# Two attentions' first batch started ahead of the pipeline, its maxima over five banks, and a last expert that writes finished rows

## What is computed

```python
x = x + tanh(g_xattn[0]) * L0_xattn(layernorm(x), ctx, ctx, mask, ...)   # causal
x = x + tanh(g_ffn[0])   * L0_ffn(layernorm(x), ...)                     # 32 experts, top 8, capacity 256
x = x + tanh(g_xattn[1]) * L1_xattn(layernorm(x), ctx, ctx, mask, ...)   # not causal
x = x + tanh(g_ffn[1])   * L1_ffn(layernorm(x), ...)                     # 8 experts, top 2, capacity 1024

def xattn(q, k, v):
    att = softmax((q @ Wq + bq) @ (k @ Wk + bk).T / sqrt(16) + mask)     # per head
    return (att @ (v @ Wv + bv)) @ Wp + bp
def L1_ffn(x):
    for each expert e, for the up to 1024 tokens routed to it:
        y[token] += gate * (relu(x[token] @ w1[e] + b1[e]) @ w2[e] + b2[e])
```

## Time and profile before

| | |
|---|---|
| median of 3 executions | 2030.68 us (2028.8 to 2036.93) |
| the profiled execution | 2030.42 us |
| its span on the core | 2028.6 us |
| TensorE busy | 1761.9 us (87%) |
| VectorE busy | 1013.3 us (50%) |
| ScalarE busy | 886.9 us (44%) |
| GpSimd busy | 795.0 us (39%) |
| mean DMA rate | 110 GB/s |

### The profile page before, as it was taken

The page is one execution under the profiler, slowest core; times in us unless marked ns, Lnnn a source line. Parts: engine busy times, 40 slices in busy tenths (PEclk is TensorE's granted clock), DMA queues, the critical chain, the costliest instruction groups (busy, mean ns, idle before and its releaser), DMA issues. The chain is left out here.

```text
span 2028.6 us, 29697 instructions
## 1 busy us (share of the span) xinstructions
PE 1761.9 (87%) x10299; PEld 1053.1 (52%) x10299; DVE 1013.3 (50%) x2630; ACT 886.9 (44%) x1684; POOL 795.0 (39%) x772
## 2 busy tenths in 40 slices
PE   3799999998846998558999999999955999999995
PEld 1456556655535877423344444443332666666664
DVE  4556666667465544218777777777420122212221
ACT  3367666665622222132777777766731111111110
POOL 4222376665634777522121233111123234433322
PEclk8899999999978999887999999999976999999998
DMA  3535556344226888534323442331132133333314
GB/s 110 173 121 164 154 167 178 113 142 125 77 78 160 171 171 171 82 119 150 96 79 94 127 140 79 113 110 60 45 97 92 26 79 84 83 78 80 82 21 104
DMA packets 210675, 223.00 MB, mean 110 GB/s; under 512 B 39870, under 2 KB 201663, under 8 KB 209863
## 3 DMA queue, kind: packets, MB, share of 16 engines
q1 hardware_dynamic: 176746, 177.54, 29.0%
q0 software_dynamic: 33792, 43.71, 11.9%
HBM read 155.10 MB, written 87.06 MB: 119 GB/s over the span
## 5 line engine op out<-in xcount | busy, mean ns | idle before, releaser
L914 DVE TENSOR_REDUCE nmx<-mxb 128x1 f32<-128x512 f32 (+1 forms) x896 | 522.2, 609 | 253.7 <-PE mxb L685 147.2
L772 ACT ACTIVATE pt<-stb 128x512 f32<-128x512 f32 x832 | 475.0, 598 | 257.2 <-PE stb L705 128.9
L685 PE MATMUL mxb<-kst,qst 96*128 96x512 bf16 (+4 forms) x1024 | 335.3, 350 | 32.6 <-DVE nmx L914 21.5
L702 PE MATMUL stb<-qst,kst 99*128 99x512 bf16 (+4 forms) x1024 | 326.0, 343 | 7.1 <-DMA qst<-m3T 4.4
L718 PE MATMUL ob<-pt,va 128*32 128x512 f32 (+3 forms) x2048 | 219.4, 523 | 2.7 <-ACT pt L772 1.7
L1245 POOL DMA_INDIRECT slots<-number,place x192 | 189.5, 987 | 58.6 <-issue 57.9
L702 PEld LDWEIGHTS stb<-qst,kst 102*128 102x128 bf16 (+1 forms) x1024 | 99.1, 99 | 215.0 <-ACT pt L772 134.3
L1768 POOL DMA_INDIRECT x_after_l<-e_y,e_token x64 | 99.5, 1555 | 271.9 <-DVE e_y L1733 257.2
L1215 POOL TENSOR_TENSOR qk<-qk,parts 128x512 f32<-128x512 f32 x64 | 72.9, 1161 | 336.6 <-ACT qk L807 224.8
L685 PEld LDWEIGHTS mxb<-kst,qst 99*128 99x128 bf16 (+1 forms) x1024 | 101.4, 99 | 146.5 <-DVE nmx L914 73.4
L1531 POOL DMA_INDIRECT x_after_l<-e_y,token x64 | 104.4, 1631 | 46.9 <-DMA x_after_l<-e_y,token 19.8
(11 more groups left out here) (258 smaller groups left out, 2891.3 us busy)
## 6 DMA issues: line engine op xcount, KB each, us to landing
qk_parts<-parts SPq DMA_DIRECT2D x16, 1536.0 KB, 6.5
qst<-qk_parts SPq DMA_DIRECT2D x384, 64.0 KB, 2.3
kst<-qk_parts SPq DMA_DIRECT2D x384, 64.0 KB, 2.2
rows<-rows SPq DMA_DIRECT2D x15, 1060.0 KB
crow<-in_ctx SPq DMA_DIRECT2D x16, 512.0 KB, 3.8
x_after_l<-xres SPq DMA_DIRECT2D x16, 512.0 KB, 3.3
e_gu_nat<-in_L_ffn_gate_up_proj SPq DMA_DIRECT2D x64, 128.0 KB
qst<-in_L_ffn_w SPq DMA_DIRECT2D x8, 1024.0 KB, 7.3
```

The lines of the kernel that those rows point to most:

```text
L685: last = pe.matmul(out, qst[par][0:rows_used, h, qt * P:(qt + 1) * P], kst[par][0:rows_used, h, 0:nk], start=True, stop=not causal)
L702: last = pe.matmul(bank[:, to:to + S - q_from(kt)], kst[par][0:ROWS, h, kt * P:(kt + 1) * P], qst[par][0:ROWS, h, q_from(kt):S], start=Tru ...
L772: act.activation(pt[:, slot(b, u), q0:S], stb[no % N_ST][:, q0:S], ACT.Exp, scale=SCALE).then_inc(s["st_free"], 1)
L914: last = dve.tensor_reduce(nmx[:, qt, h:h + 1], got[:, at:at + k_to(qt)], AX.X, ALU.max, negate=True)
```

## The change

`ITERATIONS` starts at -2 in both attentions. All of batch 0's projections stand ahead of the pipeline, in the order c, k, x, q, v (`first` on TensorE, the calls before the loop on ScalarE); k gets two of the `stb` banks and q and v one `work` bank each. k's split is ScalarE's and GpSimd's as before, q's is ScalarE's and VectorE's (`split_first`). k's half of the parts is stored on its own, then q's (`first_store`), and each stack now reads k before q. All four stacks of batch 0 stand on SP right behind that, with batch 2's x behind the first. The first half of batch 0's shift moves from behind batch 1's second stack to behind its first.

The maxima of batch 0 go round five banks, the two of `mxb` and the three of `stb` (`max_bank`); the first score of an attention waits until all maxima of batch 0 are read (`EARLY`).

In layer 0 the loads come in the order k, biases, q, v; the gates are loaded by ScalarE's queue; the second pair of stacks' ones (`w_ones1`), the empty rows and batch 0's residual stand behind batch 0's stacks; VectorE does the statistics of batch 0 ahead of the constants and the bias after batch 1's statistics (`set_up_bias`), and GpSimd fills one of the three `va` tiles first.

In `experts1` the copy to the output starts when seven experts are added. For the last one GpSimd gathers the sums so far (`gather_sums`), VectorE adds them to the gated result in one instruction, and GpSimd writes finished rows into the output (`write`), after the copy has landed.

Before, eight adds (L1768) stood in the place of the last two rows. The core of the diff:

```diff
-        ITERATIONS = range(-3, B + 2)
+        ITERATIONS = range(-2, B + 2)
+        def max_bank(n, u):
+            i = MAX_NO[u]
+            if n == 0 and i < EARLY:
+                ring = (*mxb, *stb)
+                return ring[i % len(ring)], i - len(ring) + 1
+            return mxb[i % N_MX], N_MAX * n + i - N_MX + 1
...
+            def first_store():
+                for side, ready, stored in ((1, s["lo_k"], s["k_out"]), (0, s["lo_q"], s["parts_out"])):
+                    sp.wait_ge(ready, 1)
+                    sp.dma_start(qk_dram[0][side]..., parts[:, side, :, :, :]...).then_inc(stored, 16)
...
+            first_store()
+            for g in range(GROUPS):
+                stack(0, g)
+                if g == 0:
+                    load_x(2)
+            if layer == 0:
+                sp.dma_start(kst[1][ROW_SHIFT:ROW_SHIFT + 3, :, :], ones).then_inc(a.w_ones1, 16)
+                sp.dma_start(qst[1][ROW_MASK:ROW_MASK + 3, :, :], ones).then_inc(a.w_ones1, 16)
+                empty_store(c, sp, empty)
             load_residual(0)
...
                 if nn is not None:
                     parts_store(nn)
                     stack(nn, 0)
+                if nxt == 0:
+                    shift(nxt, 0)
...
+                if no == 0:
+                    pe.wait_ge(s["max_free"], EARLY)
...
+            def first():
+                for kind in ("c", "k", "x", "q", "v"):
+                    for t in range(2):
+                        for part in range(2 if kind in TWO_PARTS else 1):
+                            trip(kind, 0, t, part)
...
+            def split_first():
+                dve.wait_ge(evac["q"], 2)
+                dve.wait_ge(s["hi_q"], 1)
+                for cc in range(NC):
+                    last = dve.tensor_tensor(qk[:, 0, cc, :], qk[:, 0, cc, :], parts[:, 0, 0, cc, :], ALU.subtract)
+                last.then_inc(s["rest_q"], 1)
+                dve.wait_ge(s["mid_q"], 1)
+                for cc in range(NC):
+                    last = dve.tensor_tensor(parts[:, 0, 2, cc, :], qk[:, 0, cc, :], parts[:, 0, 1, cc, :], ALU.subtract)
+                last.then_inc(s["lo_q"], 1)
...
-            sp.wait_ge(s["added"], 16 * TILES * E1)
+            sp.wait_ge(s["added"], 16 * TILES * (E1 - 1))
             sp.dma_start(out, x[0:T, :]).then_inc(s["copied"], 16)
...
+            def gather_sums(b):
+                pool.wait_ge(s["picked"], at(2, b, 2))
+                pool.wait_ge(s["added"], 16 * TILES * (E1 - 1))
+                for i in range(TILES):
+                    pool.indirect_dma_start(sums[:, i, :], None, x, ...).then_inc(s["sum_in"], 16)
+            def write(b):
+                pool.wait_ge(s["copied"], 16)
+                for i in range(TILES):
+                    pool.wait_ge(s["y_done"], at(TILES, b, i + 1))
+                    pool.indirect_dma_start(out, ..., y[b[1]][:, i, :], None, ...).then_inc(s["written"], 16)
```

More of the change, by code:

```diff
@@ L542, in _ @@
                     load_ctx(nn + 1)
-                if n3 is not None and n3 + 1 < B:
+                if n3 is not None and 2 < n3 + 1 < B:
                     load_x(n3 + 1)
@@ L563, in _ @@
                     store_rows(prev)
+                if layer == 0 and cur == 0:
+                    sp.wait_ge(c.empty_out, 16)
                 if layer == 0 and cur is not None:
@@ L583, in bank_free @@
             def bank_free(kind, b, t):
-                bank = BANK[kind, t]
+                if kind == "k" and b == 0:
+                    return
+                bank = t if kind in ("q", "v") and b == 0 else BANK[kind, t]
                 if held[bank]:
@@ L734, in _ @@
                 pe.wait_ge(c.tables, 2)
-                pe.wait_ge(c.made, 3)
+            first()
+            if layer == 0:
+                set_up()
             for it in ITERATIONS:
@@ L755, in _ @@
                         kind, k, t, part, _ = TRIPS[u]
[L756 removed]
+                        if item(it, k) is not None and (kind != "list" or layer == 0 and item(it, k) >= LISTED) and (kind not in FRONT or item(it, k) > 0):
                             trip(kind, item(it, k), t, part)
@@ L796, in evacuate @@
                         act.wait_ge(a.va_ones, 1)
+                    if layer == 0 and t == 0 and 0 < b < 3:
+                        act.wait_ge(a.va_ones, b + 1)
                     if t == 0 and b > 2:
@@ L853, in _ @@
                 constants_scalar(c, act)
-                act.wait_ge(a.b_in, 32)
+            evacuate("c", 0, 0)
+            evacuate("c", 0, 1)
+            for i in range(NT):
+                norm1_apply(0, i)
+            evacuate("x", 0, 0)
+            evacuate("x", 0, 1)
+            if layer == 0:
+                act.wait_ge(a.b_in, 48)
+            evacuate("k", 0, 0)
+            evacuate("k", 0, 1)
+            evacuate("q", 0, 0)
+            evacuate("q", 0, 1)
+            middle(0, 1)
+            middle(0, 0)
+            evacuate("v", 0, 0)
+            evacuate("v", 0, 1)
             for it in ITERATIONS:
                 prev, cur, nxt, nn, n3 = (item(it, k) for k in range(-1, 4))
-                if layer == 0 and it == -1:
-                    act.wait_ge(a.w_ones, 64)
+                nn = nn or None
+                if layer == 0 and it == 0:
                     act.wait_ge(c.empty_out, 16)
@@ L1117, in _ @@
             if layer == 0:
+                dve.memset(c.mhalf[:, :], -0.5).then_inc(c.half_set, 1)
                 dve.memset(m3T[0][:, :], 1.0).then_inc(a.stack_ones, 1)
-                constants_vector(c, dve, ii, empty)
             else:
                 dve.memset(base[:, :, :], 0.0).then_inc(a.zeroed, 1)
+            for i in range(NT):
+                norm1_stats(0, i)
+            norm1_mean(0)
+            if layer == 0:
+                constants_vector(c, dve, ii, empty)
+                set_up()
+            split_first()
             for it in ITERATIONS:
                 done, prev, cur, nxt, nn, n3 = (item(it, k) for k in range(-2, 4))
-                if layer == 0 and it == -2:
-                    set_up()
                 for u in range(STEPS):
+                    if layer == 0 and it == -2 and u == 14:
+                        set_up_bias()
                     if nxt is not None and u in MAX_BANKS:
@@ L1249, in _ @@
                 constants_gpsimd(c, pool, ii)
+                pool.memset(va[0][:, :, :, :], 1.0).then_inc(a.va_ones, 1)
+            norm1(0)
+            rest(0, 1)
+            low(0, 1)
             for it in ITERATIONS:
-                if layer == 0 and it == -2:
-                    for i in range(3):
-                        last = pool.memset(va[i][:, :, :, :], 1.0)
-                    last.then_inc(a.va_ones, 1)
                 done, prev, nn, n3 = item(it, -2), item(it, -1), item(it, 2), item(it, 3)
+                nn = nn or None
                 for u in range(STEPS):
+                    if layer == 0 and it == -2 and u == 15:
+                        for i in range(1, 3):
+                            pool.memset(va[i][:, :, :, :], 1.0).then_inc(a.va_ones, 1)
                     if layer and done is not None and u in (0, 16, 18, 24):
@@ L1743, in iteration @@
                 hidden(cur, 1, (1, 3, 5, 7))
-                result(cur, 0)
+                result(cur, 0, not nxt)
                 if nxt:
@@ L1747, in iteration @@
                     hidden(nxt, 0, (1, 3, 5, 7))
-                result(cur, 1)
+                result(cur, 1, not nxt)
             pipeline(dve, E1, prologue, iteration)
@@ L1773, in iteration @@
                     gather(nxt)
-                add(cur)
+                    add(cur)
+                else:
+                    gather_sums(cur)
+                    write(cur)
             pipeline(pool, E1, gather, iteration)
-            pool.wait_ge(s["added"], 16 * TILES * E1)
+            pool.wait_ge(s["written"], 16 * TILES)
 def program(nc, a, out):
```

136 lines of the change are left out of this document (85 added, 51 removed).

## The result

The changed kernel took 1980.92 us (median of four runs, 1979.48 to 1982.58), the kernel before 2030.59 in the same job: the ratio is 0.9745, with a 95% interval from 0.9728 to 0.9761. That is 49.7 us less, where 53 were forecast.

A forecast was written before the change was run, and what follows sets the result against it. Chains bound both attention heads before first scores, and the result's copy ran alone at the end; TensorE bound from the first scores on. Gains 21.6 + 16.5 + 15.0 = 53.1 us gave 1977 us, range 1963 to 1992.

The forecast's parts named there:

- first attention, to the first scores: Head of the first attention: following SP's queue, first scores at 84.8 instead of 106.37, gain 21.6 us (15 to 30).
- second attention, block to first scores: Head of the second attention: maxima 9.0 us earlier, then 44.5 instead of 52.0 to first scores; gain 16.5 us.
- the end, from the second down projection of expert 8: Program's end: the result's copy runs under expert 8, saving 15.7 us and up to 1.6 more; 15.0 with the stall.
- stall: Under expert 8: wait for the gather of the sums, taken as 1.0 us, with ends 0 and 5.
- everything between, carried over: Iteration 0 to the last add: taken as unchanged; the forecast is wrong if these stretches change in length.
- the train: SP, first attention: ones, empty rows and residual stand ahead of batch 1's parts, which the first scores' shift waits for.
- Rival A: First attention: SP's queue doesn't bind, first scores at 77.3, 7.5 us earlier; 1970 us, chance 0.13.
- rival B: Second attention: the five banks give nothing because TensorE's projections stand between the maxima; 7.5 us later, 1985, chance 0.11.
- the upper bound: Program's end: up to 1.6 us more if a plain write is cheaper than an add; end's range 11 to 17.3.
- rival C: Program's end: the gather comes so late that TensorE stands for 6 us; 1982 us, chance 0.05.
- D: Both heads: the first stack starts no earlier, only the end's gain is left; 2015 us, chance 0.03.
- E: Both iterations 0: shorter heads leave TensorE at the lower of its two clocks; 2079 us, chance 0.02.

The follow-up runs named there:

- the two repeats: The changed kernel and the kernel before, each run once more unaltered: 1980.11 us and 2031.62 us (one run).
- e4: Changed kernel with the second pair of ones, the empty rows and batch 0's residual issued ahead of batch 0's parts in the first attention: 1976.64 us.
- e6: Changed kernel with batch 0's first shift behind batch 1's second stack again: 1988.11 us.
- e5: Changed kernel with batch 0's maxima in two banks again, without the first score's wait for all of them: 1987.39 us.
- e9: Changed kernel with the edits of e2, e4 and e8 (7 matmuls), and batch 1's statistics ahead of batch 0's q split: 1962.19 us.
- e8: Changed kernel with 20 additional matmuls whose result nobody reads, where TensorE stands idle in the second attention: 1974.41 us.
- e2: Changed kernel without GpSimd's drain at the end of the last block: 1977.08 us.
- e1: Changed kernel with the last block as before the change (the last expert adds, the copy follows all adds): 1993.65 us.

## Why the prediction was right, and where its terms were off

The forecast held in place and sign, and by 3.9 us in size. The terms, in us, by the two first profiles and by the two repeats:

| term | forecast | first pair | repeats |
|---|---|---|---|
| first attention, to the first scores | 21.6 | 20.5 | 21.5 |
| second attention, block to first scores | 16.5 | 13.5 | 16.8 |
| the end, from the second down projection of expert 8 | 15.0 (16.0, less 1.0 of stall) | 12.2, without the stall | 12.1, without the stall |
| everything between, carried over (the stall in it) | 0 | 2.8 | -1.6 |
| spans | 53.1 | 49.0 | 48.7 |

**First attention.** The forecast followed SP's queue, and each of its stations is in the trace: the first stack at 31.67 (31.5 forecast), the fourth stack over at 57.3 (56.5), batch 1's parts in at 76.42 (75.1), first scores at 85.91 (84.8). That the train binds is shown by e4, and that the shift's place counts by e6. The banks buy nothing here, as forecast (e5). Rival A, a queue that doesn't bind, falls for the kernel as it is. Its time for the first scores, 77.3, is what e9 reached once the train and the statistics were out of the way. One term was badly off and cost nothing: the forecast had VectorE's maxima over near 74, ten us ahead of the shift, from first maxima at 41.5. They started at 44.25 and were over at 83.81, so 2.1 us of slack were left, and in e4 the first scores already wait for them.

**Second attention.** Here the first pair fell 3 us short, and it did so ahead of the maxima: they start 44.2 us after the block, where 40.0 were forecast. Two terms were too small. The q split was to be over 24.0 us after the block and was over after 25.9; k took 6.50 where 3.52 and 1.95 had been taken. And q's two halves with the copy between were taken at 7.0, from a place where the clock rose halfway; now TensorE had stood for 8.45 us, both halves ran at the lower clock, and it took 9.4 from the first to the maxima (874.19 to 883.54). e8 shows that the idle time is the cause. The repeats, 16.8, show that it is a matter of the execution too, in both kernels, and don't confirm the forecast's 16.5: of the 3.3 us more, 2.6 lie in the kernel before, which took longer in its repeat. Between statistics and q the forecast had 8.95 and it took 8.97 (865.22 to 874.19). From maxima to scores it had 44.5 and 43.3 were measured; VectorE's work is the bound there and the banks made it so (e5: 51.3 without them), so rival B falls.

**The end.** The copy, 15.6 us (2012.92 to 2028.56), went as forecast; the last write lands 2.29 us after issue (1972.00 to 1974.29) where the add took 3.87, which is the 1.6 of the upper bound. The gather was held up by the copy and landed at 1953.7, 19.4 us after the copy's issue, where 18.9 were worked out; the stall was 0.39, not 1.0, and rival C falls. The step that failed is the one that wasn't written: that behind the last landing nothing stands. Its sign was missed with it: the end was to come within 5 us of the last write's issue and came after 7.6. In the kernel before only 0.5 us lay between the copy's landing and the end, because GpSimd's drain was hidden under the copy. With the copy gone it stands alone, 4.96 us, and e2 takes it away: 17.0 us would have been the end's worth. The Trainium skill ("VectorE: DVE Perf Modes", section "The DRAIN you can't avoid") puts the drains of a program's preamble and postamble at about 12 ns on every engine; SP's at the end of this block is as short (7 ns), GpSimd's, which the block itself brings and e2 takes out, is not (4417 and 4961 ns).

**Rivals D and E.** The heads moved, and both iterations 0 ran at 0.95 and 0.97 of the clock: neither came.

**What was carried over** was not exactly nothing: +2.8 in the first pair, -1.6 in the repeats. Of the first, 2.9 is the clock of the last stage. That luck hid part of the miss at the end. The prediction made a change of these stretches its sign of being wrong; they did change, but by less than the 4.3 us (474.0 to 478.3) by which one of them differs between kernels that are the same there.

## What to carry to other kernels

When a long transfer at the end goes away, look up what else each engine does between its last instruction and the program's end: a drain or a wait that ran under it is now the end, and no timeline of operations shows it. When a head is a chain, follow the one queue through all its stations, as here SP's; its times came within 1.3 us, while the durations of matmuls behind an idle stretch were off by up to a factor of two. Work that a later item needs (here batch 1's statistics) belongs ahead of work that only the current item's slower path needs, if its input is there.

## What the runs showed of the hardware

GpSimd's drain at the end of the last block takes 4.3 to 5.0 us (4309 ns in e1, 4417 before, 4961 after), also when all its DMAs have landed. A gather on the software queue gets little through beside a copy in packets of 64 KB: its packets of 4 KB took turns with the copy's, one for one, and 32 of 256 had started when the copy's last ones had. The granted clock of a stage can differ between executions of one kernel by enough for 3 us (0.80 in the repeat and 1.00 in the first profile of the changed kernel, over the last stage of the second attention). And the column of the granted clock says nothing at a program's start: the trace's records of it begin at 30.0 us in the kernel before and at 16.7 in the changed one, and ahead of them the column reads 1.00, while eight transposes take 1.94 us at 17.88 before and at 8.75 after, and 1.04 at 17.53 after, behind the first record:

```profile
8.75 1.94 PE L640 MATMUL work<-ident,crow 128*128 128x128 f32 x8 [8.75 <-DMA crow<-in_ctx]
...
17.53 1.04 PE L640 MATMUL work<-ident,xn 128*128 128x128 f32 x8
```
